# Two graph attentions with their steps in another order, context and projection in two halves of a buffer, on one Trainium2 core

## What is computed

```
x = x + L0_gnn(layernorm(x), adj)   # 4 heads of 32, softmax over the neighbours, projection, LayerNorm of the result
x = x + L0_ffn(layernorm(x))        # 8 experts, the best 2 weighted
x = x + L1_gnn(layernorm(x), adj)   # 8 heads of 16, softmax over the neighbours, projection
x = x + L1_ffn(layernorm(x))        # 30 times: h + 0.01 tanh(h), silu, LayerNorm, linear
```

```
attn = einsum(q, k) * scale;  attn = where(adj == 0, -1e9, attn);  attn = softmax(attn)
out  = einsum(attn, v) @ Wo.T + bo
# first attention only: out = LayerNorm(out) * gamma + beta
```

## Time and profile before

| | |
|---|---|
| median of 3 runs | 2956.6 us (2956.55 to 2957.52) |
| profiled execution, its own time | 2959.04 us |
| its span | 2957.2 us |
| first attention, about | 24 to 470 us of the span |
| expert block | 470 to 986 us |
| second attention | 986 to 1632 us |
| recurrent block | 1632 to 2957 us |
| busy share of the span | TensorE 93%, VectorE 86%, ScalarE 72%, GpSimd 59% |

### The profile page before, as it was taken

One profiled execution on the slowest core, in us unless ns is written; L12 is line 12 of the kernel. 1 busy time (PEld: TensorE's weight loads), 2 busy tenths in 40 slices (PEclk: granted clock), 3 DMA queues, 4 the chain that ended last, 5 costly groups with the idle time before them and its releaser, 6 DMA issues. The chain is left out here.

```text
span 2957.2 us, 69168 instructions
## 1 busy us (share of the span) xinstructions
PE 2741.3 (93%) x20318; PEld 1788.0 (60%) x20447; DVE 2534.7 (86%) x6982; ACT 2127.1 (72%) x4032; POOL 1742.3 (59%) x1152
## 2 busy tenths in 40 slices
PE   5888885999999799999988799999999999999999
PEld 3555554888888465565555555555555555555556
DVE  4777775888888577777776899999999999999999
ACT  4666662444444355555554899999999999999994
POOL 2566554333333223332232499999999988888882
PEclk9999996999999899999999999999999999999999
DMA  5000000000000000000000255555555555555555
GB/s 145 22 21 18 21 8 15 1 0 0 0 0 0 23 16 14 14 14 11 14 15 2 98 197 198 198 200 200 200 200 199 197 196 197 195 196 197 198 199 172
DMA packets 132585, 281.78 MB, mean 95 GB/s; under 512 B 11760, under 2 KB 69152, under 8 KB 132512
## 3 DMA queue, kind: packets, MB, share of 16 engines
q1 hardware_dynamic: 115616, 272.44, 26.8%
q10 hardware_dynamic: 16896, 8.39, 1.0%
HBM read 270.49 MB, written 10.29 MB: 95 GB/s over the span
## 5 line engine op out<-in xcount | busy, mean ns | idle before, releaser
L1363 POOL TENSOR_TENSOR xn_sb<-xn_sb,d_rb 128x1024 f32<-128x1024 f32 x464 | 1084.2, 2372 | 154.5 <-DMA d_rb<-d_rstd_rows 154.5
L1516 PE MATMUL d_p_y<-xn_sb,d_w_main 128*128 128x512 f32 x1856 | 952.6, 595 | 0.0
L1530 PEld LDWEIGHTS d_p_gt<-ident,xn_sb 128*128 128x128 f32 x3840 | 438.8, 140 | 560.1 <-ACT xn_sb L1570 447.6
L1395 DVE BATCH_NORM_STATS2 d_stats<-d_p_gt 128x6 f32<-128x256 f32 x1920 | 713.4, 408 | 0.0
L1570 ACT ACTIVATE xn_sb<-d_th,d_bias 128x512 f32<-128x512 f32 x928 | 666.8, 719 | 13.1 <-DVE d_th L1388 0.9
L1388 DVE SCALAR_TENSOR_TENSOR d_th<-d_th,d_p_y 128x512 f32<-128x512 f32 x960 | 635.4, 662 | 4.1 <-ACT d_th L1566 3.9
L1566 ACT ACTIVATE d_th<-d_p_y,d_bias 128x512 f32<-128x512 f32 x928 | 625.1, 674 | 0.0
L1530 PE MATMUL d_p_gt<-ident,xn_sb 128*128 128x128 f32 x3840 | 584.4, 275 | 9.5 <-DVE d_stats L1395 8.6
L1098 DVE SCALAR_TENSOR_TENSOR x_sb<-m_p_y,m_combine,x_sb 128x128 f32 (+1 forms) x1024 | 311.0, 343 | 68.5 <-PE m_p_y L1140 51.8
L237 POOL TENSOR_TENSOR a_rstd<-a_var,minus_half 128x4 f32<-128x4 f32 x64 | 65.5, 1023 | 486.6 <-DVE a_var L347 484.9
L1187 ACT ACTIVATE m_hidden<-m_p_h,m_cols 128x512 f32<-128x512 f32 x256 | 176.4, 689 | 226.0 <-PE m_p_h L1132 225.9
(11 more groups left out here) (213 smaller groups left out, 3915.6 us busy)
## 6 DMA issues: line engine op xcount, KB each, us to landing
d_rb<-d_rstd_rows SPq DMA_DIRECT2D x464, 512.0 KB, 5.5
a_adj_in<-in_adj_dram SPq DMA_DIRECT2D x64, 256.0 KB, 2.8
out_dram<-d_out_sb ACTq DMA_DIRECT2D x32, 256.0 KB, 2.6
d_rstd_rows<-d_rstd_row SPq DMA_DIRECT2D x116, 16.0 KB, 1.4
m_w_sb<-in_L_ffn_w_dram SPq DMA_DIRECT2D x2, 512.0 KB
x_sb<-in_x_dram SPq DMA_DIRECT2D x1, 256.0 KB, 2.9
a_w_raw<-in_L_gnn_Wq_dram SPq DMA_DIRECT2D x2, 64.0 KB, 2.2
a_w_raw<-in_L_gnn_Wk_dram SPq DMA_DIRECT2D x2, 64.0 KB, 2.1
```

What stands on the lines that cost most here:

```text
L1363: nc.gpsimd.tensor_tensor(g[:, c, :], g[:, c, :], rb[:, buf, :], ALU.mult).then_inc(s_gs, 1)
L1395: ins = nc.vector.bn_stats(stats[:, q % 2, (j * CT + t) // 2].rearrange("p a s -> p (a s)"), p_gt[:, t * P:(t + 2) * P].rearrange("p (a c) ...
L1516: nc.tensor.matmul(p_y[:, c % 2, cols(u)], w_main[:], g[:, c, cols(u)], start=True, stop=True).then_inc(s_y, 1)
L1530: ins = nc.tensor.transpose(p_gt[:, t * P:(t + 1) * P], g[:, c, t * P:(t + 1) * P], ident[:])
```

## The change

Both attentions keep every operation. What changes is the order on each engine and the number of buffers:

- `context_t` and `proj` have two halves, chosen by `par`, so `normalise_context` waits for the projection of one quad earlier, and so does the copy of the projection.
- First attention: `transpose_x` moves from behind the sums to the end of the quad and from bank `p_z` to `p_x`; `transpose_prob` 1 goes to `p_z`. ScalarE normalises x behind the copies of probabilities 2 and 3 and of q. VectorE normalises the projection in one piece behind `stats_x`. GpSimd's `deviation_x` stands before its three passes.
- Second attention: GpSimd's `normalise_result(k)` waits in addition until the even maxima of quad k + 3 have been copied. The projection is cut behind its second graph and the even maxima are transposed in between; the sums stand ahead of the context product; `transpose_prob` 1 moves behind the odd scores; the odd sums are cut in two with the shift in between; VectorE waits for the normalised result behind the odd maxima.

```diff
-        context_t = sb("context_t", [P, QUAD])
+        context_t = sb("context_t", [P, 2, QUAD])
-            proj = sb("proj", [P, QG, P])
+            proj = sb("proj", [P, 2, QG, P])
...
                 def normalise_result(k):
                     pool.wait_ge(s_rvar, k + 1)
                     wait(pool, s_rn, k)
+                    if live(k + 3):
+                        pool.wait_ge(s_mtc, 2 * (k + 3) + 1)
...
                     if live(k + 2):
                         edges(k + 2, par)
+                    if live(k + 3):
+                        deviation_x(k + 3)
                     if live(k - 3):
                         x_quad = x_sb[:, bass.ds((k - 3) * QG, QG), :]
...
-                    if live(k + 3):
-                        deviation_x(k + 3)
...
-                def normalise_context(k):
+                def normalise_context(k, par):
                     dve.wait_ge(s_pv, PARTS * (k + 1))
                     dve.wait_ge(s_rden, k + 1)
-                    wait(dve, s_o, k)
-                    nc.vector.tensor_tensor(context_t[:], p_x[:], rden[:], ALU.mult).then_inc(s_ctx, 1)
+                    wait(dve, s_o, k - 1)
+                    nc.vector.tensor_tensor(context_t[:, par], p_x[:], rden[:], ALU.mult).then_inc(s_ctx, 1)
...
                     if live(k):
                         maxima(k)
-                    if live(k - 3):
-                        normalise_projection(k - 3, 0)
-                    if live(k):
                         take_maxima(k, p_w)
-                    if live(k - 3):
-                        normalise_projection(k - 3, 1)
                     if live(k - 1):
                         invert_sums(k - 1)
-                        normalise_context(k - 1)
+                        normalise_context(k - 1, 1 - par)
                     if live(k + 3):
                         stats_x(k + 3)
+                    if live(k - 3):
+                        normalise_projection(k - 3, 1 - par)
                     if live(k - 2):
-                        stats_projection(k - 2)
+                        stats_projection(k - 2, par)
...
-                def sum_prob(part):
+                def sum_prob(part, first=0, end=QG):
+                    columns, graphs = slice(first * P, end * P), slice(first, end)
                     for t in range(4):
-                        last = nc.tensor.matmul(p_y[tile(t), :], ones[:, part, :], prob_t[:, t],
-                                                start=part == 0, stop=part == PARTS - 1)
+                        last = nc.tensor.matmul(p_y[tile(t), columns], ones[:, part, :], prob_t[:, t, graphs],
+                                                start=part == 0 and first == 0, stop=part == PARTS - 1 and end == QG)
...
                         sum_prob(0)
-                    if live(k + 2):
-                        transpose_x(k + 2, p_z)
                     if live(k):
                         transpose_maxima(k, p_w)
...
-                        transpose_prob(k, 1, p_x)
+                        transpose_x(k + 2, p_x)
...
-                        project(k - 2, p_z)
+                        project(k - 2, par, p_z, (0, 1))
                     if live(k - 1):
                         pe.wait_ge(s_ptc, 4 * n)
                     if live(k):
                         transpose_maxima(n, p_w)
-                    if live(k - 1):
-                        pe.wait_ge(s_v, k)
-                        context_product(1 - par, 1, (0, 1))
+                    if live(k - 2):
+                        project(k - 2, par, p_z, (2, 3))
                     if live(k):
                         shift_scores(n)
                     if live(k - 1):
-                        context_product(1 - par, 1, (2, 3))
                         sum_prob(1)
+                        pe.wait_ge(s_v, k)
+                        context_product(1 - par, 1, range(QG))
...
-                        sum_prob(0)
+                        sum_prob(0, 0, 2)
                         shift_scores(n)
+                        sum_prob(0, 2, 4)
```

More of the change, by code:

```diff
@@ L671, in second_body @@
                         transpose_prob(n, 0, p_z)
+                    n = 2 * k + 1
+                    if live(k):
+                        scores(k, par, 1)
                         if live(k + 1):
@@ L674, in second_body @@
                         else:
[L675 to L680 removed]
+                            pe.wait_ge(s_mtc, n)
+                        transpose_prob(n - 1, 1, p_w)
                         pe.wait_ge(s_ptc, 4 * (n - 1) + 1)
```

80 lines of the change are left out of this document (39 added, 41 removed).

## The result

The changed kernel takes 2860.8 us (median of 4 runs, 2859.0 to 2860.9) against 2956.8 for the one before on the same chip: a ratio of 0.9673, 95% interval 0.9657 to 0.9690, or 96 us less. The profiled execution took 2859.0 with a span of 2857.1; the span of before was 2957.2, so 100.1 us went between the two spans, where the prediction had 75.6.

The account below looks back on a forecast made before the run. TensorE was taken as the bound in both attentions, its waits as what could be won: 42.2 us in the first plus 33.4 in the second, 75.6 together, bringing the median from 2956.6 to 2881 us, range 2869 to 2912.

Parts of the forecast that it names:

- I take 11.45 for the two together: First attention: beat set by TensorE at 11.3 and VectorE at 11.4 us, down from 12.96; 42.2 us less.
- 19.16 - (8.7 + 11.7 + 9.0) / 26.6 = 18.05: Second attention: beat once TensorE's waits for even maxima, odd maxima and copied x go; 33.4 us less.
- (1): First attention, ScalarE: probability copies ahead of normalising x remove TensorE's 8.9 us wait, 0.4 a quad.
- (3): First attention: two halves of context_t remove TensorE's 20.0 us wait for the context, 0.9 a quad.
- (2): First attention: moving transpose x starts the reciprocal about 1 us sooner, removing its 7.7 us wait, 0.35 a quad.
- (4): Second attention: GpSimd's LayerNorm of the result leaves the maxima splitting; 0.86 us off most quads, beat 18.68 from this alone.
- (5): Second attention: cutting the projection to transpose even maxima sooner helps remove the 8.7 us wait, 0.33 a quad.
- (6): Second attention: transpose 1 behind the odd scores removes TensorE's 9.0 us wait for copied x, 0.34 a quad.
- (7): Second attention: odd sums cut around the shift; the 11.7 us wait for odd maxima goes, 0.44 a quad.
- one: First attention: VectorE's loop closes at about 12.4 because GpSimd holds the offset or normalisations; 2908 us, chance 0.20.
- Two: Second attention wins only the lock, other waits turning up at ScalarE's next copy; beat 18.68, 2900 us, chance 0.12.
- Three: First attention: GpSimd keeps the port between instructions, holding VectorE through the third pass; beat 15.2, 2986 us, chance 0.03.

Follow-up runs that it names:

- e16: Changed kernel with two of the four normalisations of the projection left out on VectorE in the first attention's loop: 2861.8 us.
- e4: Kernel before with only the two halves of the context's buffer added: 2918.6 us, ratio 0.9872.
- e9: Changed kernel with the first part of the second attention's odd sums in one piece again, ahead of the shift: 2861.6 us.
- e15: Changed kernel without the product that puts the bias into the projection, in both attentions: 2856.2 us.
- e11: Changed kernel with the second attention's context product ahead of the second part of the even unit's sums again: 2888.5 us.
- e6: Changed kernel with the first attention's normalisation of the projection cut into halves around the copy of the maxima again: 2901.8 us.
- e13: Changed kernel with GpSimd's deviation of x behind its three passes on the projection again, first attention: 2962.3 us, ratio to the kernel before 1.0012.
- e12: Changed kernel with the second transposes of the even unit ahead of the odd scores again, second attention: 2888.1 us.
- e3: Kernel before with only the LayerNorm passes of the result moved behind the copy of the odd maxima, second attention: 2941.2 us, ratio 0.9950.
- e17: Changed kernel with one buffer of the projection again in the first attention: 2896.5 us.

## Why the prediction was right in kind and too small in size

The gain of 100.1 us between the spans against 75.6 forecast: 24.5 are missing, in three terms. The mechanism was right; three sizes in the sum were not. VectorE was taken to close the first attention at 11.4 and did not. The waits of TensorE were taken to give back their recorded length (12.96 - 1.64, and 19.16 - (8.7 + 11.7 + 9.0) / 26.6), and they gave back more. And the quads outside the counted beats were taken at nothing.

**"I take 11.45 for the two together": 6.6 us.** The step "Does VectorE close the loop later than that?" said yes, at 11.4, by putting 0.5 to 0.9 on top of 10.5. One quad of the changed kernel, VectorE and GpSimd in order of time:

```profile
256.83 1.11 DVE L430 TENSOR_SCALAR a_proj_n<-a_proj,a_stats_o,a_rstd_o 128x128 f32<-128x128 f32 x4
...
257.01 1.07 POOL L237 TENSOR_TENSOR a_rstd<-a_var,minus_half 128x4 f32<-128x4 f32 x1 [2.93 <-DVE a_var L350]
...
258.05 1.27 POOL L283 TENSOR_TENSOR a_proj_n<-a_proj_n,a_gamma 128x512 f32<-128x512 f32 x1
...
258.85 0.50 DVE L423 TENSOR_SCALAR a_var_o<-a_stats_o 128x4 f32<-128x4 f32 x1
259.26 0.15 DVE L356 SCALAR_TENSOR_TENSOR a_offset<-a_stats,a_rstd 128x4 f32<-128x4 f32 x1
259.40 1.27 POOL L285 TENSOR_TENSOR a_proj_n<-a_proj_n,a_beta 128x512 f32<-128x512 f32 x1
259.73 2.48 DVE L371 TENSOR_REDUCE a_row_max<-a_p_s 128x4 f32<-128x512 f32 x4 [0.31 <-PE a_p_s L509]
```

The order that the prediction worked out is what happened: the four normalisations are not held by the power beside them, the variance is held by the first pass to its end, the offset slips in before the second. Only the hold is 0.33 over the free instruction and not 0.5 to 0.9, and behind the offset VectorE waits 0.31 for the scores, so it is not VectorE's loop that closes. e16 shows it by itself. This allowance, 11.45 over the floor of 11.3, is 4.2 us of the 6.6.

The rest is the floor. "11.3 if nothing is lost" was TensorE's busy time before, 253.36/290 of 12.96; now it is 237.05/240 of 11.22, 11.08. Two errors in it nearly cancel, which is luck. First, the trace before lacks the matmul record of the bias product (L567) in 31 of 32 quads of each attention, and its time stands as a wait. TensorE around the projection, before and after:

```profile
260.88 0.65 PE L516 MATMUL a_p_w<-ident,a_prob 128*128 128x128 f32 x4
261.65 0.10 PEld L567 LDWEIGHTS a_p_y<-a_bias_rows,a_ones_bf 128*128 128x128 bf16 x1 [0.36 <-DVE a_rden L385]
```

```profile
255.06 0.65 PE L516 MATMUL a_p_w<-ident,a_prob 128*128 128x128 f32 x4
255.55 0.38 PE L571 MATMUL a_p_y<-a_bias_rows,a_ones_bf 128*128 128x512 bf16 x1
255.76 1.05 PE L573 MATMUL a_p_y<-a_w_o,a_context_t 128*128 128x128 f32 x8
256.66 0.60 PE L516 MATMUL a_p_z<-ident,a_prob 128*128 128x128 f32 x4
```

Before, the transposes end at 261.53, the bias product's weights are loaded at 261.65, and the projection starts 0.23 later, at 261.88; the product takes these 0.23. So of the 0.35 a quad that the prediction read as the wait for the reciprocal only about 0.12 was a wait, and the floor without any wait was 11.5 and not 11.3.

Second, a wait takes more with it than its length. Four transposes are recorded with 0.65 us, but the next product starts 0.49 behind their start when nothing holds it (255.06 to 255.55), and 0.89 behind that of a projection of 1.05 (e4). Ahead of a wait the record runs to its end, and the wait is counted from there. So TensorE is best counted from start to start. Means over the steady quads, from its order of time, beside what the earlier trace rows give as waits:

| from start to start, us a quad | before | after | waits in the rows |
|---|---|---|---|
| first: product of q to sums | 1.41 | 0.96 | 0.40 |
| first: transposes, projection, to the next transposes | 2.97 | 1.60 | 1.24 (0.22 are the bias product) |
| first: sums to transposed maxima, and last transposes to mask, with those of x counted in | 2.03 | 2.08 | none |
| second: last transposes over the bias to the projection (V) | 1.20 | 1.19 | 0.60 (0.23 are the bias product) |
| second: projection to transposes of x | 3.86 | 3.38 | 0.33 |
| second: transposes of x to odd scores, with transposes 1 counted in | 2.88 | 2.38 | 0.34 |
| second: product of k to transposed odd maxima | 1.47 | 1.06 | 0.44 |

In the first attention 1.77 go where the rows have 1.42 of true waits. The third row grows because TensorE now stands about 0.2 for the split maxima (1.20 from the sums to their transposes, where ready work follows in 0.99), under the end of the sums, so that no row of PE names it. This is the new wait at the split that the prediction called its most likely failure; it is there and small.

**"19.16 - (8.7 + 11.7 + 9.0) / 26.6 = 18.05": 8.1 us.** The three waits went, as forecast, and 1.38 us went with them, not 1.11. By the table, the place of the even maxima gave back 0.48 for 0.33, that of the copied x 0.50 for 0.34, and that of the odd maxima 0.41 for 0.44; both surpluses lie where transposes or the projection stood ahead of the wait. "What stays is the wait for V (0.6)" was right as a number: 1.20 and 1.19 from start to start. But here too a part of it is the bias product. Before has weight loads of it and no matmul:

```profile
L567 PEld LDWEIGHTS a_p_z<-a_bias_rows,a_ones_bf x27: 94/95/96, 1060.5 to 1560.1; 128*128 128x128 bf16 x27
```

After has the record:

```profile
1251.12 0.39 PE L571 MATMUL a_p_z<-a_bias_rows,a_ones_bf 128*128 128x512 bf16 x1 [0.30 <-ACT a_v_sb L766]
1251.35 0.61 PE L573 MATMUL a_p_z<-a_w_o,a_context_t 128*128 128x128 f32 x4
```

and its wait is 10.5 us in 28 quads, 0.37. e9, with the same beat within 0.01, has no such record, and its wait reads as before:

```profile
PE a_p_z L573 <- ACT a_v_sb L765: 16.5, 28, 0.7
```

that is 0.59. The end of the range, 17.8 "if half of the wait for V goes too", is the beat that came, but not for that reason: by luck. And the wait for V isn't what holds the beat: in e15 the bias product goes and the beat stays. What holds it is the way that runs through both engines. VectorE in the changed kernel, from the even split on:

```profile
1251.69 0.17 DVE L378 SCALAR_TENSOR_TENSOR a_split<-a_row_max,a_split 128x16 bf16<-128x16 f32 x1
...
1254.04 3.36 DVE L388 RECIPROCAL a_rden<-a_p_y 128x512 f32<-128x512 f32 x1 [0.55 <-PE a_p_y L554]
...
1257.49 0.69 DVE L394 TENSOR_TENSOR a_context_t<-a_p_x,a_rden 128x512 f32<-128x512 f32 x1
...
1258.10 2.47 DVE L371 TENSOR_REDUCE a_row_max<-a_p_s 128x4 f32<-128x512 f32 x4
...
1260.81 0.17 DVE L378 SCALAR_TENSOR_TENSOR a_split<-a_row_max,a_split 128x16 bf16<-128x16 f32 x1
```

and TensorE transposes what the two splits made at 1251.92 and 1261.05, 0.06 and 0.07 us behind their ends. Even scores, maxima, shift, sums, reciprocal, context, odd maxima, shift, context product, mask, scores: each starts as soon as the one before it is handed over. That is why the sums' place (e11) is worth 0.87 and the projection's bias nothing.

**The quads outside the counted beats: 9.8 us.** I priced 28 and 30 beats, but each attention has 32 quads. The fill and the drain became shorter too: 3.3 us up to the fourth quad of the first attention and 1.6 behind the last copy of the earlier trace rows; in the second 3.8 us on the first beat (1004.33 to 1024.59 before, 951.28 to 967.76 after) and 1.1 behind the last. 6.6, 8.1 and 9.8 make the 24.5. In the medians 20 us are missing, since the profiled execution before was 2.4 us above its median and the one after 1.8 below.

Of the single steps: (1) right, and 0.60 when undone. (3) right, the largest by far, and undersized (1.24 for 0.9). (2) right as to its place, but two thirds of its 0.35 were the bias product, and e6 and e13 show that it hangs on the move of the deviation ahead of the passes, to which the prediction gave no price. (4) right: 18.62 for 18.68. (5) right: 0.30 for the cut. (6) right that the wait goes, at less than half of what it is worth (0.34 for the 0.77 of e12). (7) right that the wait for the odd maxima goes and that the cut costs nothing, but e9 shows that the cut isn't what takes it away. "The sums, put ahead of the context product" had no term of its own. As for the rivals: one (beat 12.4) did not occur; the variance was held for 0.33 and the offset for nothing. Two (18.68) is e3 and not the whole change. Three did not occur: GpSimd let VectorE through after every instruction.

The rule weighed in the prediction (Trainium skill, "SBUF — State Buffer", "Who interferes with whom": the shared port pair is an exclusive lock between VectorE and GpSimd) is borne out for the 128x512 passes: the variance above ends 0.03 us behind the pass. For the 128x4 power it isn't: four normalisations beside it take 1.11 us in all, no more than twice the 0.60 of the earlier trace rows. And beside the 1.94 us of GpSimd's mask in e6 two pairs of them take 0.99 and 0.94 where they took 0.60: slowed, but not shut out for its whole length.

## What to carry to other kernels

A wait in the profile is not what its removal is worth: it can hide an instruction without a record, and it takes the tail of the product ahead of it along. Count TensorE from start to start, at the same place in a kernel or a quad where nothing waits. The same step with its neighbours undone can cost as much as the whole change wins (e13): price the place of an instruction together with what it waits for on the next engine, or don't price it alone. When TensorE is near its full share, ask of each instruction whether it is on the ring of both engines; the bias product was not, and the sums were. Count fill and drain of every stage among the quads that a change shortens.

## What the runs showed that I had not expected

The cost of two misplaced steps doesn't add: 41 and 101 us apart, 12 together. And the clock: in e17 TensorE waits for the split 18 times between 110 and 340 us, up to 1.5 us a time, and the granted clock stays at full, 2.4 GHz; in e13, with waits of up to 4.0, the same stretch has a mean grant of 0.90, so a part of it ran at 1.2 GHz. The wait of e17 and the stretch of e13:

```profile
PE a_p_w L540 <- DVE a_split L378: 26.1, 18, 1.5
```

```profile
110.00:340.00 230.00, 186.01 (x1871) 119.88 (x1868) 159.78 (x302) 130.23 (x257) 119.16 (x94) 0.90 0.06 17
```
